# Final layer norm of the first 1024 tokens in two parts, with evictions of the second half between them

## The chip, the cores and the metric

The kernel runs on the 8 cores of one Trainium2 chip. Each core computes 2048 of the 16384 tokens by itself (half of one of four sequences); the cores do not talk to each other. The metric is the time of the slowest core in microseconds (us). TensorE (PE) multiplies, VectorE (DVE) and ScalarE (ACT) do elementwise work, GpSimd (POOL) does some of it and issues DMAs, SyncE (SP) only issues DMAs.

## The reference, cut to what matters

```python
x = layernorm(x + attn(x))        # linear attention (elu+1), 16 heads, 4 kv heads, then Wo
x = layernorm(x + ffn(x))
# ffn: h = gelu(x @ q(w1).T + b1); out = h @ q(w2).T + b2
#      q(w) = sign(w) * (|w| >= 0.7 * mean|w|)       ternary weights
# shapes: x [4, 4096, 2048], w1 [8192, 2048], w2 [2048, 8192]
```

The part of interest is the last product, `h @ q(w2).T`, and the last layer norm. The sum `x + ffn(x)` is called z below.

## The kernel before

A core goes through attention, the first layer norm and the first FFN product, and parks its hidden values in HBM (`hd`). x1, the result of the first layer norm with b2 added, lies in HBM as `x1s`.

**The second product.** The 2048 tokens are taken in two halves s = 0, 1 of 1024; the 2048 output columns in four groups g of 512; a half is two blocks P = 0, 1 of 512 tokens, each four chunks of 128. One pass is (s, g, P): 256 matmuls (line 856) that fill four PSUM banks, one per chunk; P = 0 uses banks 4 to 7 and P = 1 banks 0 to 3. Numbered p = 8s + 2g + P, pass p begins in a bank when the eviction of pass p - 2 from that bank is done (semaphore `v_z`). The last two passes (s = 1, g = 3) are done chunk by chunk (line 870).

**An eviction** `evict_z(s, g, c)` has the number i = 32s + 8g + c; z32 below is the first of half 1. VectorE adds the bank to a 128x512 tile `zt(i)` that holds x1 (line 1098), then takes its statistics (line 1100). There are two such tiles, in turn. `load_x1r` on ScalarE's queue (line 1239) fills one from `x1s`; it waits until the tile's last z has been stored. `store_z` on POOL's queue (line 597) writes the tile to `zs` in HBM. So z34 needs in turn: z32 evicted, z32 stored, x1 for z34 loaded. Pass 8 yields z32 to z35, pass 9 z36 to z39, pass 10 z40 to z43.

**The layer norm of half 0.** When its 32 evictions are done, VectorE aggregates the statistics (line 1106), ScalarE makes the reciprocal deviations, and eight chunks of 128x2048 are read back from `zs`, normalised on VectorE (line 1128) and written out. Three buffers serve in turn (`zre(c)`). POOL's queue issues it all: the loads of chunks 0 to 2 (line 621), and then for each chunk c the output store (line 624), a wait until that store has landed, and the load of chunk c + 3 (line 627). For c = 5, 6, 7 there is nothing left to load and no such wait.

**Order.** Each engine carries out its instructions in the order in which the program writes them. On VectorE and on POOL all eight chunks of the layer norm stood before the first eviction and the first store of half 1. Meanwhile TensorE runs passes 8 and 9, whose banks were freed by the last evictions of half 0. SP reloads the ternary W2 for the next column group, a quarter at a time (line 505), as pass P = 1 has finished with it.

Of the kernel before, what the change touches and what calls it, by code (L numbers as in the profile page):

```python
# [77 lines left out]
W1_PRE = 4  # L78
PRE_ITEM = [48, 52, 56, 60]
PRE2_QUAD = [40, 43, 46, 49, 52, 55, 58]  # L80
W2_PRE = 7


def build_nc():
# [144 lines left out]
    def zt(i):  # L229
        return mcf[:, 2048 + (i % 2) * 512: 2048 + (i % 2 + 1) * 512]  # L230

    def w2q_sb(s, g, q):
        if s == 0 and g == 0 and q < W2_PRE:
            o = 2 * q * KB if q < 4 else (2 + 2 * q) * KB
            return mb8[:, o:o + 2 * KB]
        return r38[:, q * 2048:(q + 1) * 2048]
# [44 lines left out]
    def zre(c):  # L281
        return stage(c % 3)
# [3 lines left out]
    def st(c, g):  # L286
        return stats[:, (c % 8) * 24 + g * 6:(c % 8) * 24 + (g + 1) * 6]
# [95 lines left out]
    def w2_stage(r):  # L383
        if r < W2_PRE:
            return w2_slot7
        j = (r - W2_PRE) % 3
        return maf[:, j * 2048:(j + 1) * 2048] if j < 2 else mcf[:, 0:2048]

    def w2_signal(r):
        return d_s7 if r < W2_PRE else (d_st[0], d_st[1], d_mc)[(r - W2_PRE) % 3]  # L390

    def w2_load_no(r):
        if r < W2_PRE:
            return 16 * (r + 1)
        j = (r - W2_PRE) % 3
        return 16 * ((N_ST[j] + 32 if j < 2 else 0) + (r - W2_PRE) // 3 + 1)
# [6 lines left out]
    def sync_program(e):  # L403
# [35 lines left out]
        def load_half(u):  # L439
            if u < 2:  # L440
                e.wait_ge(a_abs, NW_FULL)
            elif u == 2:
                e.wait_ge(t_tr, 2 * NCH)
            else:
                e.wait_ge(a_abs, NW_FULL + u - 2)
            e.dma_start(out=stage_half(u), in_=w_half(u)).then_inc(d_h[u % 3], 16)
# [5 lines left out]
        def load_w2(r):  # L452
            if r == 0:
                e.wait_ge(d_x1[2], 16 * 5)
            elif r < W2_PRE or r >= W2_PRE + 3:
                e.wait_ge(v_w2, r if r < W2_PRE else r - 2)
            elif r < W2_PRE + 2:
                e.wait_ge(v_w1, 63 + r - W2_PRE)
            else:
                e.wait_ge(t_m, n_m(63, M3))  # L460
                e.wait_ge(p_q, n_qs(31, Q2))
            e.dma_start(out=w2_stage(r), in_=w2h[r // 16, r % 16]).then_inc(w2_signal(r), 16)

        for u in range(NU):
            for h in w_behind_u(u - 1) if u >= 1 else ():
                if h + 3 < NW_HALF:
                    load_half(h + 3)
            if u + 2 in PRE2_QUAD:
                load_w2(PRE2_QUAD.index(u + 2))
            if 5 + u < NFC and u >= 1:  # L470
# [50 lines left out]
    def gpsimd_program(e):  # L521
# [72 lines left out]
        def store_z(s, g, c):  # L594
            i = s * 32 + g * 8 + c
            e.wait_ge(v_z, i + 1)
            e.dma_start(out=zs[s * 8 + c, :, g * 512:(g + 1) * 512], in_=zt(i)).then_inc(d_zs[i % 2], 16)  # L597
# [24 lines left out]
        for c in range(8):  # L622
            e.wait_ge(v_ln, c + 1)
            e.dma_start(out=out[c * 128:(c + 1) * 128, :], in_=zre(c)).then_inc(d_o1[c % 3], 16)
            if c + 3 < 8:
                e.wait_ge(d_o1[c % 3], 16 * (c // 3 + 1))
                e.dma_start(out=zre(c + 3), in_=zs[c + 3]).then_inc(d_zl[c % 3], 16)
        for g in range(3):
            for c in range(8):
                store_z(1, g, c)  # L630
        for c in range(8):
# [245 lines left out]
    def vector_program(e):  # L877
# [50 lines left out]
        def begin_threshold(no):  # L928

            b = N_THR[no] + no  # L930
            if no == 0:
                e.wait_ge(a_abs, 64)
                res = wres[:, 0:64]
                e.tensor_scalar(res, wsum[:, 0:64], -K2048, None, ALU.add).then_inc(v_thr)
            else:
                nf = NW_FULL - 64
                res = wres
                e.wait_ge(a_abs, NW_ALL)
                e.tensor_scalar(res[:, 0:nf], wsum[:, 64:NW_FULL], -K2048, None, ALU.add).then_inc(v_thr)
                e.tensor_scalar(res[:, nf:], wsum[:, NW_FULL:], -K2048 / 2, None, ALU.add).then_inc(v_thr)  # L940
            e.wait_ge(v_thr, b + 1)
            e.reduce_sum(thr[:, 6:7], res, mybir.AxisListType.X).then_inc(v_thr)
# [36 lines left out]
        def tern_w2(g, q):  # L979
            r = g * 16 + q  # L980
            e.wait_ge(w2_signal(r), w2_load_no(r))
            if g >= 1:
                if q == 0:
                    e.wait_ge(d_w2s[(g - 1) % 2], 256 * ((g - 1) // 2 + 1))
                if q < 15:
                    e.wait_ge(t_w2, 15 * (g - 1) + q + 1)
                else:
                    e.wait_ge(t_z, 8 * g)
            elif q == 0:
                e.wait_ge(a_abs, NW_ALL)  # L990
            elif q == W2_PRE:
                e.wait_ge(t_m, n_m(62, M3))
            ternary(w2q_sb(0, g, q), w2_stage(r), 1, n_tern[0], v_w2)
            last_tern[0] = (v_w2, r + 1)
            n_tern[0] += 1
# [62 lines left out]
        def sum_m3(u):  # L1058
            e.wait_ge(t_m, n_m(u, M3))
            e.tensor_tensor(tq(u, 2), PB[m_bank(u, M3)], tq(u, 2), ALU.add).then_inc(v_q)  # L1060
            e.wait_ge(v_q, n_q(u, VH2))
            e.tensor_tensor(tq(u, 0), PB[m_bank(u, M3)], tq(u, 0), ALU.add).then_inc(v_q)

        for u in range(NU_CL, NU):
# [23 lines left out]
            if u == THR2_QUAD - 1:  # L1088
                begin_threshold(1)
            if u in PRE2_QUAD:  # L1090
                tern_w2(0, PRE2_QUAD.index(u))
        sum_m3(NU - 1)

        def evict_z(s, g, c):
            i = s * 32 + g * 8 + c
            e.wait_ge(t_z, i + 1)
            e.wait_ge(d_zt[i % 2], 16 * (i // 2 + 1))
            e.tensor_tensor(zt(i), PB[F2_BANK[c // 4][c % 4]], zt(i), ALU.add).then_inc(v_z)  # L1098
            e.wait_ge(v_z, i + 1)
            e.bn_stats(st(c, g), zt(i)).then_inc(v_bz)  # L1100
# [25 lines left out]
        for c in range(8):  # L1126
            e.wait_ge(d_zl[c % 3], 16 * (c // 3 + 1))
            e.tensor_scalar(zre(c), zre(c), mv[:, 2 * c:2 * c + 1], rstd[:, c:c + 1],
                            ALU.subtract, ALU.mult).then_inc(v_ln)
        for g in range(3):  # L1130
            for c in range(8):
                evict_z(1, g, c)
        for c in range(8):
# [200 lines left out]
    with nc.Block() as block:  # L1334
        block.sync(sync_program)
        block.gpsimd(gpsimd_program)
        block.vector(vector_program)
        block.scalar(scalar_program)
        block.tensor(tensor_program)
# [57 lines left out]
```

## Time and profile before

| | us |
|---|---|
| median of 3 runs | 2494.3 |
| lowest, highest of them | 2493.86, 2610.59 |
| profiled execution | 2497.7 |
| its span on core 6, the slowest | 2496.2 |
| spans of the 8 cores | 2480.4 to 2496.2 |
| TensorE busy, core 6 | 2406.0 |
| VectorE busy | 1246.5 |
| ScalarE busy | 725.6 |
| POOL busy | 551.4 |

A span is the time from a core's first instruction to its last. Busy times are sums over all stages. A row of a timeline has the start in us, the length in us, engine, line of the kernel, operation, output and inputs with shapes, count, and in brackets how long the engine had stood before it and what released it. DMA-issuing instructions count as a moment of their engine; the time until the data has landed is told apart.

### The profile page before, as it was taken

The numbers are of one execution on the slowest core, as the hardware profiler recorded it, in microseconds if no ns is written. First come the engines' busy times: TensorE is split into PE (matmuls) and PEld (weight loads), VectorE is DVE, ScalarE is ACT, GpSimd is POOL, SyncE is SP. The second block draws the span as 40 slices with busy tenths as digits, with TensorE's granted clock in tenths as the row PEclk, the third lists the DMA queues.
The fourth block names the chain that finished last, engine by engine and source line by source line (L and its number), as shares of the span: only waits on it lengthen the run. The fifth ranks groups of instructions, "written<-read, shape, count | busy, mean of one in ns | idle before, by whom it ended". The sixth has DMA issues, their size and how long they took to land.

```text
span 2496.2 us, 31950 instructions; the slowest of 8 cores (2480.4 to 2496.2 us)
## 1 busy us (share of the span) xinstructions
PE 2406.0 (96%) x11300; PEld 1094.4 (44%) x11300; DVE 1246.5 (50%) x1395; ACT 725.6 (29%) x1109; POOL 551.4 (22%) x419
## 2 busy tenths in 40 slices
PE   4999999999999999999999999799999999799997
PEld 1444444444444444444444444344444444344443
DVE  1222344445567777777788886375747211200021
ACT  0233477743323666666433333000000000000000
POOL 3000000004336334344343433011212000100000
PEclk9999999999999999999999999899999999899999
DMA  9994688696655887787544446976848577522253
GB/s 159 217 239 153 157 203 204 165 268 241 232 223 181 265 263 254 258 265 265 188 144 165 160 144 234 327 243 216 277 151 287 180 254 238 173 68 68 85 194 118
DMA packets 106955, 507.01 MB, mean 203 GB/s; under 512 B 12976, under 2 KB 12976, under 8 KB 69808
## 3 DMA queue, kind: packets, MB, share of 16 engines
q1 hardware_dynamic: 50400, 323.55, 38.9%
q0 software_dynamic: 27600, 124.80, 19.1%
q10 hardware_dynamic: 28800, 56.64, 7.3%
q8 instruction: 93, 1.52, 0.2%
q14 instruction: 62, 0.51, 0.1%
HBM read 444.11 MB, written 98.57 MB: 217 GB/s over the span
## 4 chain that ended last, share of the span: by engine, by line
PE 87%; DMA 10%; DVE 2%; issue 1%; POOL 0%; ACT 0%; SPq 0%; DVEq 0%; POOLq 0%; ACTq 0%
PE PB L767 29%; PE PB L856 25%; PE PB L694 8%; PE PB L731 8%; PE PB L870 4%; PE PB L668 4%; PE PB L658 4%; PE PB L758 2%; DMA MA<-w2h 2%; DMA out<-MA 2%; DMA R<-woh 2%; DMA RW<-wvh 2%; DMA zs<-MC 1%; DMA MC<-x1s 1%; DMA hd<-R 1%
## 5 line engine op out<-in xcount | busy, mean ns | idle before, releaser
L856 PE MATMUL PB<-R 128*128 128x512 fp8e4 x2576 | 572.2, 385 | 34.2 <-DVE MC L1098 17.9
L767 PE MATMUL PB<-R,RW 128*128 128x512 bf16 x2400 | 537.6, 379 | 0.0
L856 PEld LDWEIGHTS PB<-R 128*128 128x128 bf16 x2576 | 254.6, 99 | 350.5 <-issue 55.4
L767 PEld LDWEIGHTS PB<-R,RW 128*128 128x128 fp8e4 x2400 | 234.7, 98 | 283.0
L579 POOL TENSOR_TENSOR RW<-MC 128x1024 fp8e4<-128x1024 fp8e4 x120 | 244.1, 2066 | 283.1 <-DVE MC L963 283.1
L1098 DVE TENSOR_TENSOR MC<-PB,MC 128x512 f32<-128x512 f32 x56 | 38.4, 685 | 404.6 <-PE PB L856 243.9
L694 PE MATMUL PB<-R,MB 128*128 128x512 bf16 x1024 | 231.1, 379 | 0.0
L767 PE MATMUL PB<-R,MC 128*128 128x512 bf16 x960 | 226.8, 379 | 0.0
L856 PE MATMUL PB<-R,RW 128*128 128x512 fp8e4 x784 | 170.4, 379 | 0.0
L960 DVE TENSOR_SCALAR MB<-MA,thr 128x2048 fp8e4<-128x2048 f32 x102 | 137.8, 1351 | 54.6 <-DMA MA<-w2h 40.9
L963 DVE SCALAR_TENSOR_TENSOR MC<-MA,thr,MB 128x2048 fp8e4<-128x2048 f32 x64 | 158.3, 2473 | 7.0 <-DVE MB L960 0.5
L694 PEld LDWEIGHTS PB<-R,MB 128*128 128x128 bf16 x1024 | 100.1, 98 | 120.7
L658 PE MATMUL PB<-RW,R 128*128 128x512 bf16 x512 | 121.2, 390 | 28.1 <-DMA R<-xb 28.1
L1225 ACT ACT_TABLE_LOAD x1 | 1.3, 1283 | 503.1 <-DVE mv L1106 503.1
L767 PEld LDWEIGHTS PB<-R,MC 128*128 128x128 fp8e4 x960 | 93.9, 98 | 113.3
L597 POOL DMA_DIRECT2D zs<-MC x56 | 35.3, 630 | 448.9 <-DVE MC L1098 446.1
L1153 ACT ACTIVATE MA<-MA 128x2048 f32<-128x2048 f32 x69 | 130.8, 1895 | 9.8 <-DMA MA<-w1h 9.7
L1272 ACT ACTIVATE RW<-PB 128x512 f32<-128x512 f32 x180 | 105.2, 594 | 90.2 <-PE PB L767 88.3
L1324 ACT ACTIVATE lnv<-mv,c_eps_ln 128x1 f32<-128x1 f32 x8 | 2.4, 294 | 424.1 <-DVE mv L1142 416.9
L668 PE MATMUL PB<-RW,R 128*128 128x512 bf16 x512 | 119.5, 387 | 5.8 <-DMA RW<-wvh 5.8
L1253 ACT ACTIVATE R<-RW,b_sb 128x512 bf16<-128x512 f32 x120 | 85.8, 719 | 129.6 <-DVE RW L1083 62.9
L1253 ACT ACTIVATE RW<-RW,b_sb 128x512 bf16<-128x512 f32 x120 | 86.0, 720 | 127.6 <-DVE RW L1083 64.8
(134 smaller groups left out, 2525.6 us busy)
## 6 DMA issues: line engine op xcount, KB each, us to landing
MA<-w1h SPq DMA_DIRECT2D x126, 1024.0 KB, 6.5
MB<-w2h SPq DMA_DIRECT2D x108, 512.0 KB, 7.8
MA<-w2h SPq DMA_DIRECT2D x45, 1024.0 KB, 7.8
MC<-w2h SPq DMA_DIRECT2D x19, 1024.0 KB, 7.8
R<-xb POOLq DMA_DIRECT2D x32, 512.0 KB, 78.5
x1s<-R POOLq DMA_DIRECT2D x16, 1024.0 KB, 4.6
hd<-RW ACTq DMA_DIRECT2D x64, 256.0 KB, 4.6
hd<-R ACTq DMA_DIRECT2D x64, 256.0 KB, 4.9
```

The costliest lines, as they stand in the source:

```text
L579: e.tensor_tensor(w_sum(j, k), x, y, op, saturate=False).then_inc(p_q)
L658: ins = e.matmul(PB[sc % 2], xs(blk % 4, dc)[:, cc * 128:(cc + 1) * 128], wk_sb(dc), start=(dc == 0), stop=(dc == 15))
L668: ins = e.matmul(PB[2 + sc % 2], xs(blk % 4, dc)[:, cc * 128:(cc + 1) * 128], wv_sb(dc), start=(dc == 0), stop=(dc == 15))
L694: ins = e.matmul(PB[n % 3], wq_sb(ic)[:, dc * 128:(dc + 1) * 128], x_own(t, dc), start=(dc == 0), stop=(dc == 15))
L731: ins = e.matmul(PB[WO_BANK[i % 4]], attn_chunk(c, ic), wo_sb(ic, g), start=(ic == 0), stop=(ic == 15))
L767: ins = e.matmul(PB[m_bank(u, i)], w[:, dc * 128:(dc + 1) * 128], x[:, dc * 512:(dc + 1) * 512], start=(dc == 0), stop=(dc == 7))
L856: ins = e.matmul(PB[F2_BANK[P][cc]], hid(fc, P)[:, cc * 128:(cc + 1) * 128], w2q_sb(s, g, q)[:, j * 512:(j + 1) * 512], start=(fc == 0), s ...
L960: e.tensor_single_scalar(b8t, src, thr[:, 2 * no:2 * no + 1], ALU.is_le, saturate=False).then_inc(v_b)
L963: e.scalar_tensor_tensor(dst, src, thr[:, 2 * no + 1:2 * no + 2], b8t, ALU.is_ge, ALU.subtract, saturate=False).then_inc(signal)
L1153: e.activation(stage(j), stage(j), AF.Abs, accum_out=wsum[:, i:i + 1]).then_inc(a_abs)
L1253: e.activation(hb(P, half, par), src, AF.Gelu, bias=b1_sb[:, 2 * j + par:2 * j + par + 1]).then_inc(a_h)
L1272: e.activation(tq(u, slot), PB[m_bank(u, i)], AF.Copy).then_inc(a_c)
```

## The change

On VectorE the evictions z32 to z35 stand behind the fourth chunk of the layer norm of half 0, and z36 to z39 behind the eighth; then the column groups 1 and 2 follow as before. On POOL the four stores stand behind the turn of the fourth chunk (its output store, the wait and the load of chunk 6), the other four behind the turn of the last. The instructions themselves and their counts are the same, and TensorE's, ScalarE's and SP's programs are unchanged.

```diff
+LN_FIRST = 4
...
@@ gpsimd_program
         for c in range(8):
             e.wait_ge(v_ln, c + 1)
...
             if c + 3 < 8:
                 e.wait_ge(d_o1[c % 3], 16 * (c // 3 + 1))
                 e.dma_start(out=zre(c + 3), in_=zs[c + 3]).then_inc(d_zl[c % 3], 16)
-        for g in range(3):
+            if c == LN_FIRST - 1:
+                for k in range(4):
+                    store_z(1, 0, k)
+        for k in range(4, 8):
+            store_z(1, 0, k)
+        for g in range(1, 3):
             for c in range(8):
                 store_z(1, g, c)
@@ vector_program
             e.tensor_scalar(zre(c), zre(c), mv[:, 2 * c:2 * c + 1], rstd[:, c:c + 1],
                             ALU.subtract, ALU.mult).then_inc(v_ln)
-        for g in range(3):
+            if c == LN_FIRST - 1:
+                for k in range(4):
+                    evict_z(1, 0, k)
+        for k in range(4, 8):
+            evict_z(1, 0, k)
+        for g in range(1, 3):
             for c in range(8):
                 evict_z(1, g, c)
```

## Rows read from the trace of the kernel before

**Rows 1.** The page's first part: busy time, share of the span, instructions.
```profile
PE 2406.0 (96%) x11300; PEld 1094.4 (44%) x11300; DVE 1246.5 (50%) x1395; ACT 725.6 (29%) x1109; POOL 551.4 (22%) x419
```
**Rows 2.** Chain of waits, core 6: start us, length us, what.
```profile
2136.51 8.10 DMA zs<-MC
...
2144.73 3.15 DMA MC<-x1s
...
2150.19 222.66 PE PB L856 x1021
```
**Rows 3.** What TensorE waited for, core 6: total us, times, longest us.
```profile
PE PB L856 <- DVE MC L1098: 17.9, 4, 10.8
```
**Rows 4.** Timeline of VectorE, core 6, 2000 to 2420 us.
```profile
2019.53 0.69 DVE L1098 TENSOR_TENSOR MC<-PB,MC 128x512 f32<-128x512 f32 x1 [18.12 <-PE PB L856]
...
2082.26 1.35 DVE L1128 TENSOR_SCALAR MA<-MA,mv,rstd 128x2048 f32<-128x2048 f32 x1 [9.28 <-DMA MA<-zs]
2096.14 1.35 DVE L1128 TENSOR_SCALAR MA<-MA,mv,rstd 128x2048 f32<-128x2048 f32 x1 [12.53 <-DMA MA<-zs]
...
2133.90 1.35 DVE L1128 TENSOR_SCALAR MA<-MA,mv,rstd 128x2048 f32<-128x2048 f32 x1 [11.75 <-DMA MA<-zs]
2135.16 0.69 DVE L1098 TENSOR_TENSOR MC<-PB,MC 128x512 f32<-128x512 f32 x1
...
2149.37 0.67 DVE L1098 TENSOR_TENSOR MC<-PB,MC 128x512 f32<-128x512 f32 x1
...
2206.62 0.69 DVE L1098 TENSOR_TENSOR MC<-PB,MC 128x512 f32<-128x512 f32 x1 [37.39 <-PE PB L856]
...
2261.87 0.69 DVE L1098 TENSOR_TENSOR MC<-PB,MC 128x512 f32<-128x512 f32 x1 [44.88 <-PE PB L856]
```
**Rows 5.** Timeline of TensorE, core 6: the last stretch of pass 9.
```profile
2102.72 27.79 PE L856 MATMUL PB<-R 128*128 128x512 fp8e4 x128
```
**Rows 6.** Windows, core 6: us, busy of each engine, granted clock, DMA share, GB/s.
```profile
2130.00:2150.00 20.00, 2.26 (x6) 0.32 (x4) 5.85 (x8) 0.00 (x0) 2.16 (x4) 0.60 0.79 303
2150.00:2170.00 20.00, 19.81 (x82) 8.56 (x83) 6.29 (x10) 0.00 (x0) 2.69 (x5) 0.89 0.47 125
```
**Rows 7.** Timeline of POOL's queue, core 6.
```profile
2113.89 0.53 POOL L627 DMA_DIRECT2D MA<-zs  x1 [11.48 <-DMA out<-MA]
2114.43 0.54 POOL L624 DMA_DIRECT2D out<-MA  x1
...
2135.91 0.53 POOL L624 DMA_DIRECT2D out<-MA  x1 [7.13 <-DVE MC L1098]
```
**Rows 8.** DMA issues at 2135.8 to 2136.2: count, KB, us to landing.
```profile
out<-MA POOLq DMA_DIRECT2D x1, 1024.0 KB, 7.9
```
**Rows 9.** Line 627, loads of chunks 3 to 7, core 6.
```profile
DMA to landing us min/median/max: 6.3/6.8/9.0
```
**Rows 10.** Line 1239, ten loads of x1 from 2057 us, core 6.
```profile
DMA to landing us min/median/max: 3.1/3.2/5.4
```
**Rows 11.** Core 1: POOL's store of z32, VectorE's eviction of z35.
```profile
2114.53 0.54 POOL L597 DMA_DIRECT2D zs<-MC  x1
...
2133.32 0.69 DVE L1098 TENSOR_TENSOR MC<-PB,MC 128x512 f32<-128x512 f32 x1 [3.12 <-DMA MC<-x1s]
```
**Rows 12.** Line 624, output stores of half 0, core 6.
```profile
DMA to landing us min/median/max: 5.6/11.4/13.4
```
**Rows 13.** Spans and mean granted clock of the cores.
```profile
core 0: 2491.5 us, clock 0.989
...
core 5: 2488.6 us, clock 0.988
core 6: 2496.2 us, clock 0.987
```
**Rows 14.** Timeline of VectorE, core 0: ends of passes 7 and 10.
```profile
2018.18 0.69 DVE L1098 TENSOR_TENSOR MC<-PB,MC 128x512 f32<-128x512 f32 x1 [20.93 <-PE PB L856]
...
2201.97 0.69 DVE L1098 TENSOR_TENSOR MC<-PB,MC 128x512 f32<-128x512 f32 x1 [37.93 <-PE PB L856]
```

## The prediction

> **What bounds the kernel now.** I read the page's table of busy time first: TensorE is busy for 96% of the span [rows 1]. So time can only be won where TensorE stands still or runs at its lower clock, and the question is whether this change touches such a place. The chain of waits answers it. For almost all of the last 800 us the chain is TensorE, but between 2019 us and 2150 us it leaves it for the final layer norm of the first half and comes back through one store of z, one load of x1 and the eviction behind them; then TensorE carries the chain to the end [rows 2]. The list of what TensorE waited for prices the hole: 17.9 us in four waits for line 1098, the evictions [rows 3].
>
> Next the timeline of VectorE on core 6, the slowest [rows 4]. Number the passes p = 8s + 2g + P. Pass 7 ends at 2019.53, when its first eviction runs. The layer norm then holds VectorE in order until its eighth chunk at 2133.90, each chunk short but waiting some 12 us for its load. The evictions z32 to z35 of pass 8, which free the four banks that pass 10 needs, stand behind it: z32 at 2135.16, z35 at 2149.37. TensorE finished pass 9 at 2102.72 + 27.79 = 2130.51 [rows 5] and pass 10 runs steadily only from 2150.19 [rows 2].
>
> Two rows give the whole loss, clock included. A pass without a hole takes 2261.87 - 2206.62 = 55.25 us. From the end of pass 7 to the end of pass 10 there are 2206.62 - 2019.53 = 187.09 us [rows 4] for three passes, 165.75 us. The loss is **21.3 us**: 17.9 of waiting, 3.4 of matmuls at the lower level of the clock. The granted clock shows it: 0.60 in the 20 us around the hole (nearer the level of 1.2 GHz than 2.4 GHz) and 0.89 in the 20 us behind it [rows 6], after an engine that had stood.
>
> **The change, part by part.** Nothing is added or removed; four evictions with their statistics move on VectorE from behind chunk 7 to behind chunk 3, and on POOL their four stores move from behind the last output store to behind the load of chunk 6. ScalarE's four loads of x1 keep their place, but two of them (z34, z35) wait for stores that are now earlier. SP's queue and TensorE's program are untouched, and so are all passes up to 9.
>
> *VectorE.* Chunk 3 runs at 2082.26 for 1.35 us [rows 4]. Pass 8 ended about 2019.53 + 55.25 = 2074.8, and the buffers for z32 and z33 were filled meanwhile (the loads of x1 counted from 2057 us on, each 3.1 to 5.4 us [rows 10]), so z32 and z33 go at 2083.7 and 2085.1. Then VectorE stands in order at z34 until its buffer is refilled. That needs z32's store.
>
> *POOL.* The store stands behind POOL's load of chunk 6, issued at 2113.89 [rows 7], which itself waits for the output store of chunk 3. That part of the queue is before the move and keeps its times. So z32's store is issued at about 2114.4, where the output store of chunk 4 stands now.
>
> *The round trip* store, load, eviction is the one cost that the trace shows only in other company. Nearest row: the same store of z32, issued at 2136.51, took 8.10 us and the load 3.15 us [rows 2]. The 8.10 has a reason: the output store of chunk 7, issued on the same queue at 2135.91 [rows 7], landed 7.9 us later [rows 8], at 2143.8, and z32 at 2144.6, just 0.8 us behind it. The 256 KB came home behind the megabyte ahead of it. After the change it is the load of chunk 6 that is ahead, which takes 6.3 to 9.0 us, middle 6.8 [rows 9]. So: 2113.9 + 6.8 + 0.8 = 2121.5 for the store, + 3.2 for the load [rows 10] = 2124.7, z34 there, z35 1.4 us later, ended at 2126.9. TensorE needs them at 2130.5. **Residual stall: none**, 3.6 us to spare.
> The Trainium skill (DMA: Bandwidth & Descriptors, section on queues, rings and completion order) says that a DMA engine takes turns between queues and works through one queue's ring in order; by that rule POOL's store can't pass POOL's load, the pair above agrees, and without it the store would not have to sit out the load's 6.8 us. By either the sum is the same, but only by this rule is the margin so thin; it speaks against where the stores were put.
>
> Bounds for it. Longest load ahead (9.0) and longest load of x1 (5.4): 2131.2, a stall of 0.7 us. Worst round trip of a core whose pair was slow: on core 1 from the issue of z32's store at 2114.53 to z35 at 2133.32 [rows 11], 18.8 us; from 2114.4 that makes 2133.2, ended 2133.9, a stall of 3.4 us, and again up to 3.4 for the clock. Lower end: nothing. I take nothing, since the queue ahead is then one load and not two output stores.
>
> *What is late instead.* Layer norm chunk 4 moves from 2096.14 [rows 4] to behind z35, 2126.9. Its cover: nobody but POOL waits for it. From there: chunk 1.35; output store 5.6 to 13.4, middle 11.4 [rows 12]; load of chunk 7 6.8 (6.3 to 9.0) [rows 9]; chunk 7 and evictions z36 and z37, 4.2; the round trip for z38 and z39, up to 18.8. With some 2 us for issues and core 6's own 12.9 us for the round trip: 2126.9 + 1.4 + 11.4 + 6.8 + 4.2 + 2 + 12.9 = 2165.6, a chain of 39 us; with all maxima one of 49 us, to 2175.7. Pass 11 needs the four banks at 2130.5 + 55.25 = 2185.8. Slack 10 to 20 us, or 3 where z35 is late as well, so this costs nothing. If the cover were gone it would be paid one for one in front of pass 11. Passes 12 to 15 evict as before, and the final chunks' loads wait for stores that have 200 us to land. The reload of the last quarter of W2 is issued by TensorE's own progress and is first read three quarters into pass 10.
>
> *Sum.* Core 6: 2496.2 - 21.3 = 2474.9. Core 0, the second [rows 13], lost 2201.97 - 2018.18 - 165.75 = 18.0 [rows 14] and ends at 2473.5. Core 5 (2488.6) with either loss ends at 2467 to 2471. So core 6 stays the slowest. The profiled execution took 2497.7; 2497.7 - 21.3 = 2476.4. The median of the runs shown, 2494.3, lies 3.4 below it, so the forecast is **2473 us**, 0.9% faster.
>
> **The rivals.**
> *A residual stall in front of pass 10.* For it: VectorE now stands at z34 with POOL's store behind a 1 MB load, and 3.6 us is little beside round trips that vary from 12.9 us (core 6) to 18.8 us (core 1). Against: fewer bytes ahead in the queue. 3 to 15 us plus clock: 2476 to 2491. Chance 0.17.
> *No gain: the wait only changes its name.* VectorE's order puts four chunks between z35 and z36, so pass 11 could stall as pass 10 did. For equality the chain from 2126.9 must end 21 us after 2185.8: 80 us in place of the 39 to 49 worked out. Against: every leg at its maximum stays below. Time 2490 to 2497; chance 0.05.
> *Slower than before*, by the same place: outputs, w2 reloads, z stores and x1 loads all meet after 2130, where DMA engines were already busy for 0.79 of the time [rows 6]. If every leg took twice its maximum the chain of 49 us would last 98, ending at 2225, a stall of 39 us where 21 were won: 2473 + 39 = 2512. It turns from gain to loss at 80 us. Chance 0.03.
> *More than the hole is won*, through less waiting elsewhere: behind 2150.19 TensorE runs 1021 matmuls without a break [rows 2], so below 2469 only the scatter of runs leads. Chance 0.03.
> That the change doesn't do what it says I weigh little: pass 10 waits only for the four evictions that are moved, and all they need is earlier. It is within the rivals' 0.05.
>
> **How the numbers follow.** The forecast has 0.72. Its own range is 2469 (2494.3 - 21.3, less the 3.8 between the shown runs and the profiled one) to 2480 (a stall of 3.4 and as much for the clock). To hold 8 in 10, the range takes in the lower part of the residual stall: 2468 to 2484. A change of 2% (50 us), about what a measurement of this kernel can tell from no change, can't be won from a hole of 21.3: faster 0.01. Slower by so much (2544) needs a stall of 71 us in front of pass 11, a chain of 130: 0.02, most of it for what I have not thought of. Within 2%: 0.97.
>
> **What the profile after would show.** TensorE's wait for line 1098 falls from 17.9 us to under 4; the granted clock stays at 1.00 from 2130 to 2170. On core 6, z32 and z33 run right behind the fourth chunk at 2084 and 2085, z34 and z35 at 2125 to 2130; the fifth chunk stands near 2128, the eighth near 2150; z36 to z39 are done by 2170 or so. POOL's store of z32 follows its load of chunk 6 at once and lands 7 to 9 us later. The end of pass 10 comes near 2186. The prediction fails if z34 comes after 2131 on the slowest core (the round trip was mis-sized), if TensorE waits in front of pass 11 (the moved chunks' cover was too thin), or if the hole closes and the time stays (another core or the tail sets the end).

## The result, and the profile after

The changed kernel takes 2474.2 us (median of 4 runs, the lowest 2473.1), the kernel before in the same session 2493.9 at the lowest. The ratio of after to before is **0.992, 95% interval 0.990 to 0.994**: 0.8% faster, and clearly so. In some runs of either kernel the cores of a die show a lower granted clock and the time is up to 13% longer; such runs are in the medians but not in the ratios.

The spans by core, after; [rows 13] are the rows of before. Lines are numbered as in each run's own kernel, so that the same line of code has another number below than in the rows of before.

```profile
core 0: 2472.8 us, clock 0.991
...
core 4: 2473.7 us, clock 0.991
...
core 6: 2473.9 us, clock 0.992
```

The chain of waits of core 6, cut off at 1700 us: start, length, what. Before, it ran through DMAs, VectorE and POOL between 2019 and 2150 us; now TensorE carries it without a break from 1622.56 us, in the first pass of half 0, to the last matmul.

```profile
1699.85 650.74 PE PB L862 x3015
2350.58 110.52 PE PB L876 x512
```

The windows of core 6 (busy time of PE, PEld, DVE, ACT, POOL, then granted clock, DMA share, GB/s) answer to [rows 6]. Where TensorE had 6 matmuls in 20 us it has 95, at full clock; the DMA engines are as busy as before, so it is not that the traffic went away.

```profile
2130.00:2150.00 20.00, 20.00 (x95) 9.10 (x93) 3.80 (x5) 0.00 (x0) 2.81 (x6) 1.00 0.83 292
2150.00:2170.00 20.00, 20.00 (x95) 9.00 (x94) 2.79 (x5) 0.00 (x0) 1.49 (x3) 1.00 0.44 150
```

VectorE's timeline on core 6, which answers to [rows 4] (some rows between are left out). Line 1104 is an eviction, line 1134 a chunk of the layer norm.

```profile
2018.59 0.69 DVE L1104 TENSOR_TENSOR MC<-PB,MC 128x512 f32<-128x512 f32 x1 [20.76 <-PE PB L862]
...
2081.28 1.35 DVE L1134 TENSOR_SCALAR MA<-MA,mv,rstd 128x2048 f32<-128x2048 f32 x1 [10.52 <-DMA MA<-zs]
2082.55 0.68 DVE L1104 TENSOR_TENSOR MC<-PB,MC 128x512 f32<-128x512 f32 x1
...
2083.94 0.67 DVE L1104 TENSOR_TENSOR MC<-PB,MC 128x512 f32<-128x512 f32 x1
...
2123.34 0.69 DVE L1104 TENSOR_TENSOR MC<-PB,MC 128x512 f32<-128x512 f32 x1 [37.92 <-DMA MC<-x1s]
...
2124.74 0.67 DVE L1104 TENSOR_TENSOR MC<-PB,MC 128x512 f32<-128x512 f32 x1
...
2126.13 1.33 DVE L1134 TENSOR_SCALAR MA<-MA,mv,rstd 128x2048 f32<-128x2048 f32 x1
2127.37 1.34 DVE L1134 TENSOR_SCALAR MB<-MB,mv,rstd 128x2048 f32<-128x2048 f32 x1
2128.63 1.34 DVE L1134 TENSOR_SCALAR MA<-MA,mv,rstd 128x2048 f32<-128x2048 f32 x1
2145.99 1.35 DVE L1134 TENSOR_SCALAR MA<-MA,mv,rstd 128x2048 f32<-128x2048 f32 x1 [16.02 <-DMA MA<-zs]
...
2159.34 0.67 DVE L1104 TENSOR_TENSOR MC<-PB,MC 128x512 f32<-128x512 f32 x1
...
2184.35 0.69 DVE L1104 TENSOR_TENSOR MC<-PB,MC 128x512 f32<-128x512 f32 x1 [23.55 <-PE PB L862]
```

Read it as one chain. Chunk 3, then z32 and z33; VectorE stands 37.9 us for z34's x1, which costs nothing; z35 ends at 2125.4. Pass 9 ends at 2018.59 + 2 x 55.25 = 2129.1, so the margin is 3.7 us (2.5 to 11.0 on the eight cores). Chunks 4 to 6 were loaded long since and follow in 4 us. Chunk 7 stands near 2146, z39 (2159.34) is done 24 us before pass 10 ends. And from the end of pass 7 to that of pass 10 there are 2184.35 - 2018.59 = 165.8 us: exactly three passes, where before there were 187.1. All eight cores show the same 165.8.

POOL's queue on core 6 answers to [rows 7]:

```profile
2108.71 0.53 POOL L628 DMA_DIRECT2D MA<-zs  x1 [10.53 <-DMA out<-MA]
2109.22 1.19 POOL L598 DMA_DIRECT2D zs<-MC  x2
2124.57 0.54 POOL L598 DMA_DIRECT2D zs<-MC  x1 [14.15 <-DVE MC L1104]
```

The stores of z32 and z33 took this long from issue to landing (first row); the two loads of x1 for z34 and z35, issued when they had landed, took the time of the second:

```profile
DMA to landing us min/median/max: 8.6/8.6/8.7
```

```profile
DMA to landing us min/median/max: 5.3/5.4/5.6
```

### The profile page after: what moved, and what is told of

Same layout as the page of the kernel before. It is cut to its first block, busy times and chain, and to the rows that moved or that the text cites. A ratio compares the mean times of both kernels' runs of the same rounds, so it can differ in the third digit from the quotient of the medians.

```text
span 2473.9 us, 31808 instructions; the slowest of 8 cores (2462.2 to 2473.9 us)
## 1 busy us (share of the span) xinstructions
PE 2393.8 (97%) x11158; PEld 1094.0 (44%) x11300; DVE 1243.9 (50%) x1395; ACT 725.6 (29%) x1109; POOL 552.1 (22%) x419
## 4 chain that ended last, share of the span: by engine, by line
PE 91%; DMA 6%; DVE 2%; issue 1%; POOL 0%; ACT 0%; SPq 0%; DVEq 0%; POOLq 0%; ACTq 0%
PE PB L862 29%; PE PB L773 29%; PE PB L700 8%; PE PB L737 8%; PE PB L876 4%; PE PB L674 4%; PE PB L664 4%; PE PB L764 2%; DMA MA<-w2h 2%; DMA R<-woh 2%; DMA RW<-wvh 2%; DMA hd<-R 1%; PE PB L716 1%; PE PB L689 0%; PE PB L687 0%
## 5 line engine op out<-in xcount | busy, mean ns | idle before, releaser
L969 DVE SCALAR_TENSOR_TENSOR MC<-MA,thr,MB 128x2048 fp8e4<-128x2048 f32 x64 | 158.3, 2473 | 7.0 <-DVE MB L966 0.5
```

Source lines behind the costliest of these rows:

```text
L969: e.scalar_tensor_tensor(dst, src, thr[:, 2 * no + 1:2 * no + 2], b8t, ALU.is_ge, ALU.subtract, saturate=False).then_inc(signal)
```

## The experiments

The theory: the hole in front of pass 10 was the whole of the loss; what closes it is that the *round trip* (evict z32, store it, load x1 for z34, evict z34) starts early enough, in the order of VectorE and in that of POOL's queue. Rivals: VectorE's order alone made the hole; the layer norm's traffic costs TensorE something; the moved chunks will be paid in front of pass 11; bytes ahead on POOL's queue do not matter.

e1 to e4 ran side by side. The kernel before took 2488.7 us there in the middle, 5.6 less than the 2494.3 from which the times in their expectations were worked out, and the change itself was not among them; so their ratios say more than their times. A time "in the middle" is the median of the runs that are in the ratio.

**e1: two evictions early, their stores late**

```diff
-            if c == LN_FIRST - 1:
-                for k in range(4):
-                    store_z(1, 0, k)
-        for k in range(4, 8):
+        for k in range(8):
             store_z(1, 0, k)
...
-                for k in range(4):
+                for k in range(2):
                     evict_z(1, 0, k)
-        for k in range(4, 8):
+        for k in range(2, 8):
```

> z32 and z33 are evicted behind the fourth chunk of the layer norm as in the change; their stores stay behind the last output store on POOL's queue and z34, z35 stay behind the eighth chunk. Theory (what has to come early is the whole round trip eviction, store, load, not the eviction): z32's store is issued at about 2136 us on core 6 as before, z34 follows near 2148, TensorE's wait for the evictions stays at 13 to 18 us and the time at 2490 to 2498. Rival (VectorE's order alone made the hole, and freeing two of the four banks wins half of it): wait of about 9 us, time near 2484.

Measured: ratio **0.9995 (0.9985 to 1.0005)**, 2487.3 us in the middle, TensorE's wait 12.6 to 16.4 us on the eight cores. Nothing is won though half of the banks come free some 47 us earlier. VectorE on core 4, whose pass 9 ends at 2124.7:

```profile
2078.55 0.68 DVE L1101 TENSOR_TENSOR MC<-PB,MC 128x512 f32<-128x512 f32 x1
2079.95 0.67 DVE L1101 TENSOR_TENSOR MC<-PB,MC 128x512 f32<-128x512 f32 x1
...
2124.77 1.35 DVE L1131 TENSOR_SCALAR MA<-MA,mv,rstd 128x2048 f32<-128x2048 f32 x1 [10.88 <-DMA MA<-zs]
2140.13 0.69 DVE L1101 TENSOR_TENSOR MC<-PB,MC 128x512 f32<-128x512 f32 x1 [14.01 <-DMA MC<-x1s]
```

z34 waits 14 us for a load that waits for a store issued at 2127.39. So freeing two banks by VectorE's order alone wins nothing, where that rival had half of the hole.

**e2: the same two, with their stores early**

```diff
             if c == LN_FIRST - 1:
-                for k in range(4):
+                for k in range(2):
                     store_z(1, 0, k)
-        for k in range(4, 8):
+        for k in range(2, 8):
...
```

The same two lines change on VectorE, with evict_z.

> z32 and z33 and their stores early as in the change, z34 and z35 behind the eighth chunk. Theory: their buffers are full long before, so z34 and z35 run right behind the eighth chunk, on core 6 at about 2136 and 2138 us against a pass 9 that ends near 2130: a hole of 5 to 9 us there and 0 to 4 on the others, z35's wait for a load is zero, time 2480 to 2487. Rival (the round trip does not matter, only that all four stand ahead of the eighth chunk): 2490 or more.

Ratio **0.9963 (0.9952 to 0.9974)**, 2478.2 us in the middle: not quite half of the gain that the change had in its own comparison. z34 and z35 no longer wait for a load, on any core; what is left is the lateness of the eighth chunk. TensorE waited 0 to 1.5 us on five cores and 4.2 on core 4, but 11.2 on core 0 and 15.5 on core 5, more than I expected of any. The slowest is core 5, with pass 9 ending at 2121.5:

```profile
2135.03 1.35 DVE L1134 TENSOR_SCALAR MA<-MA,mv,rstd 128x2048 f32<-128x2048 f32 x1 [14.28 <-DMA MA<-zs]
2136.29 0.68 DVE L1104 TENSOR_TENSOR MC<-PB,MC 128x512 f32<-128x512 f32 x1
```

So each queue accounts for a part: POOL's early stores are needed (e1 against e2), and so is VectorE's order (e2 against the change).

**e3 and e4: the cut behind the fifth, and behind the sixth chunk** (`LN_FIRST = 5`, `LN_FIRST = 6`)

> The change with the cut behind the fifth chunk in place of the fourth. Theory: z32's store is now issued behind POOL's load of chunk 7, at about 2127.6 us on core 6, waits for that megabyte (6.8 us) and lands near 2135; z34 near 2139, z35 at 2140: a hole of 8 to 12 us plus 2 to 3 of clock, time 2483 to 2489. Rival (POOL's queue holds nothing back, a 256 KB store lands 3 to 4 us after its issue whatever is ahead): z34 near 2134, hole 5 us, time 2478 to 2481.

> The change with the cut behind the sixth chunk. The store of z32 is issued only a microsecond later than with the cut behind the fifth, but with one more megabyte, the output store of chunk 5, ahead of it on POOL's queue. Theory (the queue's bytes ahead set the landing): z32 lands 5 us or more later than in the run before, 11 to 14 us after its issue, TensorE's wait is 13 to 18 us, time 2488 to 2496, nearly all of the gain gone. Rival (queue holds nothing back): less than 2 us more than with the cut behind the fifth chunk.

Ratios **0.9963 (0.9948 to 0.9978)** and **0.9979 (0.9965 to 0.9992)**, 2479.4 and 2483.4 us in the middle. Both times lie below what I expected, and e3's falls into the rival's 2478 to 2481; counted from the kernel before as it ran beside them, 5.6 lower, both are back in the expected ranges and e3's is out of the rival's. TensorE waited 1.8 to 4.2 us on seven cores and 10.4 on core 7 in e3; 4.7 to 17.0 in e4, where I had 13 to 18. POOL's queue on the slowest core of each, e3 core 7 and e4 core 3, with the landing of z32's store behind each:

```profile
2116.28 0.53 POOL L628 DMA_DIRECT2D MA<-zs  x1 [10.24 <-DMA out<-MA]
2116.80 1.17 POOL L598 DMA_DIRECT2D zs<-MC  x2
```

```profile
DMA to landing us min/median/max: 6.7/6.7/6.7
```

```profile
2120.73 0.53 POOL L628 DMA_DIRECT2D MA<-zs  x1 [11.81 <-DMA out<-MA]
2121.27 0.54 POOL L625 DMA_DIRECT2D out<-MB  x1
2121.89 1.14 POOL L598 DMA_DIRECT2D zs<-MC  x2
```

```profile
DMA to landing us min/median/max: 12.4/12.4/12.4
```

These two rows are far apart, 6.7 us and 12.4, but they do not stand for the rest: over the eight cores z32's store landed 8.7 us after its issue on average in e3 (6.7 to 10.7) and 11.4 in e4 (10.0 to 13.3), 2.7 us later for one megabyte more ahead. I had expected 5 us or more, so this missed. From the issue of z32's store to z34 it is 13.3 us against 17.0, 3.7 more, where the rival had under 2. In e3 the slowest core's hole (10.4) is what I expected, the other seven had far less, because their layer norm ran earlier against pass 9 than core 6's had in the trace from which I took the times.

**e7: the stores of z32 and z33 ahead of the wait and the load of chunk 6**

```diff
             e.dma_start(out=out[c * 128:(c + 1) * 128, :], in_=zre(c)).then_inc(d_o1[c % 3], 16)
+            if c == LN_FIRST - 1:
+                for k in range(2):
+                    store_z(1, 0, k)
...
             if c == LN_FIRST - 1:
-                for k in range(4):
+                for k in range(2, 4):
                     store_z(1, 0, k)
```

> The change with POOL's stores of z32 and z33 issued ahead of the wait and the load of chunk 6, right behind the output store of chunk 3 (about 2098 us on core 6). Theory by POOL's queue in order: z32 lands only about 1 us behind that output store, 8 to 14 us after its own issue, and z34 runs at 2110 to 2115, some 10 us earlier than in the change. Rival (no order on the queue): lands 3 to 4 us after its issue, z34 at 2105 or earlier. Either way the time is that of the change within 2 us.

Ratio **0.9921 (0.9904 to 0.9938)**. On core 0 the output store of chunk 3 was issued at 2095.65 and landed 10.7 us later, at 2106.4; the two small stores were issued at 2096.30 and took:

```profile
DMA to landing us min/median/max: 12.4/13.2/14.0
```

They landed behind it, not after 3 to 4 us, and z34 ran at 2115.38. From the end of z35 to the end of pass 9 the eight cores have 7.9 to 14.6 us here (11.8 on average), where the change has 2.5 to 11.0 (6.8): some 5 us of margin for a swap of two stores. In before, after, e3, e4 and e7, on all eight cores of each, z32's store landed 0.3 to 2.9 us behind the megabyte ahead of it on POOL's queue, never before it. That is what an order on the queue would give, but by itself it does not show one: e6 has the other half.

**e6: the stores of z32 to z35 on ScalarE's queue**

```diff
+        def store_z_act(k):
+            i = 32 + k
+            e.wait_ge(v_z, i + 1)
+            e.dma_start(out=zs[8 + k, :, 0:512], in_=zt(i)).then_inc(d_za[i % 2], 16)
...
+        load_x1r(1, 0, 0)
+        load_x1r(1, 0, 1)
+        for k in range(4):
+            store_z_act(k)
+            if k % 2 == 1:
+                load_x1r(1, 0, k + 1)
+                load_x1r(1, 0, k + 2)
...
```

The four stores have two semaphores of their own, and are gone from POOL's queue.

> The change with the stores of z32 to z35 issued from ScalarE's queue, where nothing is ahead of them but the loads of x1. Theory: z32's store goes at about 2084 us on core 6 and lands in 3 to 8 us, z34 runs at 2088 to 2096 in place of 2123, some 30 us earlier, and the fifth chunk keeps its old time; the time stays that of the change within 2 us, since the hole was already closed. Rival (transfers after 2130 still cost TensorE something, or the slack of 4 us was used up on some core in unprofiled runs): 3 us or more faster than the change.

Ratio **0.9920 (0.9905 to 0.9935)**, the change's. On core 4 the stores were issued at 2083.6 and 2085.0 and landed in

```profile
DMA to landing us min/median/max: 3.3/3.6/3.9
```

when POOL's megabyte of chunk 2 was just landing and nothing else of it was on its way. But the two loads of x1 behind them, with nothing large ahead on their own queue, took

```profile
DMA to landing us min/median/max: 12.6/12.7/12.7
```

and the stores of z34 and z35 did no better. On core 2 they were issued at 2099.7 and 2101.1, just behind POOL's output store of chunk 3 (2099.33, line 626); the first row is POOL's megabyte, the second the two small stores on ScalarE's queue:

```profile
2099.33 0.54 POOL L626 DMA_DIRECT2D out<-MA  x1
DMA to landing us min/median/max: 14.9/14.9/14.9
```

```profile
DMA to landing us min/median/max: 14.1/14.4/14.7
```

The first small store landed at 2114.4, 0.2 us behind the megabyte on the other queue. Over the eight cores z32's store took 3.1 to 5.6 us, z34's and z35's 5.1 to 14.7, and the twelve of these that were issued 0.2 to 3.1 us after an output store of POOL landed 0.1 to 2.8 us behind it. So a small store can wait as long on a queue that holds nothing large, and lands behind the megabyte just the same; what tells the quick stores from the late ones here is what was on its way on all queues when they were issued. That order on POOL's own queue adds to this is not shown.

On core 4 z34 ran at 2099.80, 24 us sooner than in the change (on average over the cores too; I had said 30). The margin in front of pass 10 grows to 26 us and more, and no time is won over the change, so in most runs of the change its small margin was enough (but see e12).

**e8: no layer norm of half 0** (its reads, its chunks and its output stores are left out; the first 1024 output rows are not written)

> The layer norm of half 0 is left out: its eight reads of z, its eight chunks on VectorE and its eight output stores (the first 1024 rows of the output are not written); evictions and stores of half 1 follow at once. Theory: the layer norm is fully hidden after the change, so this takes the same time as the change within 3 us, 2471 to 2476. Rival (16 MB less to move also shortens something that TensorE waits for): 5 us or more faster than the change.

Ratio **0.9919 (0.9904 to 0.9934)**, median 2474.2. The layer norm with its 16 MB of traffic is now wholly free: doing it and not doing it take the same time. And the round trip is short without it: from the issue of z32's store to z34 the eight cores took 6.0 to 8.1 us, against 12.3 to 15.9 in the change. It also runs some 30 us earlier here, when no W2 is reloaded, so not all of the difference need be the layer norm's.

**e9: the cut behind the second chunk** (`LN_FIRST = 2`)

> The change with the cut behind the second chunk in place of the fourth. VectorE then waits for the end of pass 8 and for the round trip before chunks 2 to 7. Theory (the cut only has to leave room for one round trip before pass 9 ends, and the chunks behind it are hidden): z34 runs some 20 us or more before pass 9 ends, no wait of TensorE, time that of the change, ratio 0.990 to 0.994. The eighth chunk ends where it does in the change, within 8 us, since either way one round trip is put into the chain of output stores. Rival (the more chunks stand behind the cut the later z36 to z39, and pass 11 stalls): a wait of 5 us or more in front of pass 11.

Ratio **0.9928 (0.9914 to 0.9943)**, no wait of TensorE, and a margin in front of pass 10 of 24 to 31 us. VectorE on core 0, pass 9 ending at 2130.9 and pass 10 at 2186.2:

```profile
2070.10 1.35 DVE L1134 TENSOR_SCALAR MA<-MA,mv,rstd 128x2048 f32<-128x2048 f32 x1 [1.56 <-DMA MA<-zs]
2075.67 0.69 DVE L1104 TENSOR_TENSOR MC<-PB,MC 128x512 f32<-128x512 f32 x1 [4.22 <-PE PB L862]
...
2100.43 0.69 DVE L1104 TENSOR_TENSOR MC<-PB,MC 128x512 f32<-128x512 f32 x1 [21.88 <-DMA MC<-x1s]
...
2149.94 1.35 DVE L1134 TENSOR_SCALAR MA<-MA,mv,rstd 128x2048 f32<-128x2048 f32 x1 [7.28 <-DMA MA<-zs]
```

z34 comes 30 us ahead of need, and the eighth chunk stands only 4 us later than in the change (2145.99), though six chunks are behind the cut and not four.

**e10 and e11: taking the cover from the moved chunks**

```diff
+            if c == 4:
+                e.wait_ge(d_o1[c % 3], 16 * (c // 3 + 1))
+                for k in range(4):
+                    e.dma_start(out=out[c * 128:(c + 1) * 128, :], in_=zre(c)).then_inc(d_ex, 16)
+                    e.wait_ge(d_ex, 16 * (k + 1))
             if c + 3 < 8:
```

e11 has `range(10)`.

> The change with the output store of the fifth chunk issued four times more, one after the other (same data to the same rows), before the load of chunk 7. It takes the cover from the moved chunks: four stores of 6 to 12 us each put the eighth chunk 25 to 45 us later. Theory of the slower rival (the chain is paid one for one once it passes the end of pass 10, 24 us after z39 in the change): z39 ends at 2188 to 2205 on the slowest core against 2184, a wait of 3 to 20 us in front of pass 11 and 2 to 3 us of clock, time 2478 to 2497; none in front of pass 10. Rival (the end of pass 10 is no real limit, something else would give way): the time stays within 2 us of the change.

Ratio **0.9927 (0.9907 to 0.9947)**, no wait. This one missed: the four additional stores landed 4.1 to 8.0 us after their issue, 4.1 to 4.4 on core 6, the eighth chunk stood at 2164.53 (18.5 us later), and z39 at 2177.42 on core 6 was still 5 us ahead of the end of pass 10. It says that 18 us more are free, and does not tell the theories apart. So with ten:

> As the run before, with ten further output stores of the fifth chunk in place of four, since the four took only 5 to 6 us each and left z39 6 us before the end of pass 10. Six more of 4.7 us put z36 to z39 28 us later: z39 at about 2205 us on the slowest core against the end of pass 10 at 2183. Theory (the chain is paid one for one behind that point): a wait of 18 to 26 us in front of pass 11, 2 to 3.5 us of clock, none in front of pass 10, time 2493 to 2503, slower than the kernel before. Rival (something else gives way): 2480 or less.

Ratio **1.0024 (1.0012 to 1.0036)**, slower than the kernel before. In the middle it took 2505.9 us, above the 2493 to 2503 that I expected, and the kernel before 2499.7 in that session. The slowest core, 7: its waits of TensorE and its timeline of TensorE.

```profile
PE PB L868 <- DVE MC L1110: 26.5, 4, 16.6
```

```profile
2109.68 73.76 PE L868 MATMUL PB<-R 128*128 128x512 fp8e4 x341
2200.05 0.59 PE L868 MATMUL PB<-R,RW 128*128 128x512 fp8e4 x1 [16.61 <-DVE MC L1110]
```

Nothing in front of pass 10, all of it in front of pass 11. I had expected 18 to 26 us of waiting; it is 26.5. By the pace, core 7 took 250.9 us from the end of pass 7 to that of pass 11, where four passes take 221.0: 29.9 us lost for 26.5 of waiting. The hole has only moved one pass on, as the slower rival had it.

**e5 and e12: the change again**

> The changed kernel itself, as the mark for the runs beside it. Theory: 2471 to 2476 us, ratio to the kernel before 0.990 to 0.993, no wait of TensorE for the evictions on any core. Rival (part of the gain was scatter): ratio 0.994 or more.

> The changed kernel itself beside the run above. 2472 to 2476 us, ratio 0.990 to 0.994.

Neither has enough runs for a ratio with an interval. The lowest times were 2473.8 against 2491.1 of before, and 2477.0 against 2495.3: 0.993 each; e12's lies 1 us above what I expected. In e5's profile no core waits for the evictions. In e12's, core 3 does, which is the slowest of that execution:

```profile
2130.80 0.69 DVE L1104 TENSOR_TENSOR MC<-PB,MC 128x512 f32<-128x512 f32 x1 [0.79 <-DMA MC<-x1s]
```

```profile
2131.63 54.77 PE L862 MATMUL PB<-R 128*128 128x512 fp8e4 x253 [1.90 <-DVE MC L1104]
```

POOL issued z32's store at 2115.19 there, z34 ran at 2128.5, z35 ended at 2131.5, and TensorE, whose pass 9 ended at 2017.89 + 2 x 55.25 = 2128.4, waited 1.9 us and lost 2.3 by the pace. Core 7 had nothing to spare (z35 ended at 2130.2 and pass 9 too). So over the 24 core readings of the change (after, e5, e12) the margin is -3.1 to 11.0 us: the hole is closed in most executions, and not by construction. e7 (7.9 at least) and e9 (24 at least) take the same time with more room.

## Why the prediction was right, and where it was not

The forecast time and its main mechanism held. Two steps of the working failed: the round trip, priced at 10.3 us, took 14.1; and the step that set 2% as what a measurement can tell, and by it put a gain of 0.9% beside no change, where the runs tell a gain of 0.8% to 0.2% either way. They are told below, under their names.

**The hole and its price.** Right. 21.3 us on core 6 by two rows, of which 0 is left. Forecast 2473, measured 2474.2; the spans of cores 6 and 0 were to be 2474.9 and 2473.5 and are 2473.9 and 2472.8. That they agree within 1 us is partly luck: a core's earlier stages scatter by more. Core 4 ended pass 7 at 2008.19 us before and at 2018.18 after; by the same sum it would have ended at 2481.6 - 18.1 = 2463.5, and it ended at 2473.7, beside core 6. e2, e3 and e4 put back parts of the hole and parts of the time, e1 nearly all of both.

**The clock's share.** Right: the granted clock is 1.00 in both windows, and the 3.4 us are back. Other holes show the same extra. In e2 core 0 waited 11.2 us and lost 14.0 against three undisturbed passes, core 5 waited 15.5 and lost 17.8.

**The round trip.** This term of the sum failed, and luck made up for it. I took 10.3 us from the issue of z32's store to z34; on core 6 it took 14.1 (2109.22 to 2123.34), on the eight cores 12.3 to 15.9. Two terms are off: the store landed 2.9 us behind the load ahead of it and not 0.8 (8.6 us in all), and x1 took 5.4 us and not 3.2. The trace of before had the better value: from the issue of z32's store to z34 its eight cores took 11.5 to 17.0 us, 14.1 on average, and I had gone by core 6, the shortest of them. But POOL reached the store at 2109.2 and not at 2114.4, because in this execution the layer norm began 2.2 us earlier (chunk 0 at 2064.30, before at 2066.51) and the output stores of chunks 0 to 3 took 38.7 us together and not 41.5. Up to there the two programs are the same, so that is scatter and not the change: with the queue of the trace before, 2114.4 + 14.1 + 1.4 + 0.7 = 2130.6 would have left no margin at all, and in e12 core 3 had less than none. So "3.6 us to spare" was right for a wrong reason, and the residual stall is a rival that came true in part: 1 of 24 core readings, 1.9 us, less than its 3 to 15. My bound of 18.8 us, to z35, was the right one to keep; the middle value was not.

**POOL's queue.** The observation holds, and the reason that I gave for it is not shown. z32's store landed behind the megabyte ahead of it in 40 of 40 readings, but e6's small stores and loads did the same behind megabytes on another queue, and there took up to 14.7 and 12.8 us. The Trainium skill (DMA: Bandwidth & Descriptors, section on queues, rings and completion order) says of the queues of SP and ACT that an engine consumes a ring's descriptors in order, and that this is not an order of completion; so the rule is weaker than I made it, and no run here separates it from sharing. It also says that engines take turns between queues by packets, so that e6's load of x1 shares with a megabyte on each of two others; the trace agrees that an output store, a chunk's load and a reload of W2 were on their way in that window, but which of them held the load is not shown. What is shown is that the round trip takes half the time in a moment without the layer norm's transfers (e8: 6.0 to 8.1 us).

**The moved chunks.** Right that they are free, with more slack than I said: 24 us and not 20 (z39 ends at 2160.0; I had 2165.6). e10 shows 18 us of it to be free, e11 what happens beyond. My price behind the end of pass 10, one for one, holds: on core 7 of e11 z39 ended 28.6 us behind the end of an undisturbed pass 10, and 29.9 us were lost.

**What a measurement can tell.** This step failed. I said that a change of 2% is about what can be told from no change, and so took a gain that my own sum put at 0.9% for one that would pass for none; the 0.97 on "within 2%" came true, but says nothing of that. The paired ratio has an interval of 0.2% to either side, and the 0.8% measured is clear of it. The sum was the better statement: a gain of 21 us out of 2494 was forecast with 0.72, and should have been called a gain that the runs would show.

## What to carry to other kernels

When one engine's order puts an independent stage ahead of evictions, follow the buffers of the evictions too: with two buffers it is the store and the load between the first and the third eviction that must start early, and so the order on the queue that issues the store (e1 won nothing, e2 half). Issue a small store that somebody waits for before the large transfers, not behind them; another queue helps only as far as it lets the store go at a moment when little is on its way (e6: 3.1 to 5.6 us for z32, up to 14.7 for z34). Cut the hiding stage early, for what stands behind the cut is free as long as it ends before the *next* pass needs it: the cut behind the second chunk took the same time as the one behind the fourth, with 24 us of margin at least where the other had sometimes none (e9, e12). Read a cost that varies from all eight cores and not from the one that is slowest. Price a hole by two marks of the pace around it rather than by its waits alone: here that gave 21.3 us against 17.9, and 20 came.

## What the runs showed of the hardware that was not expected

A 1 MB output store took 9.9 us in the middle (5.5 to 12.2, core 6 after) among the other traffic of the stage, and 4.1 to 4.4 us on core 6 when POOL issued nothing beside it (e10). A 256 KB load of x1 took 3.2 us in the middle of ten ([rows 10]) and 12.7 in e6, with nothing large ahead on its queue. A 256 KB store took 3.1 to 5.6 us on ScalarE's queue in a quiet moment and 14.7 in a busy one, and then landed 0.2 us behind a megabyte that had been issued 0.4 us before it on POOL's queue (e6, core 2).
